# A selective-scan and mixture-of-experts kernel: scans of two segments at once, carries injected by GpSimd, and a new order of the slots

## The reference

```
u, z   = split(xn @ W_in.T)                      # 512 channels each
u_c    = silu(causal_conv4(u) + conv_b)
dt,B,C = split(u_c @ W_xp.T, [16, 32])           # 16 states
dt     = softplus(dt @ W_dt.T + b_dt);  A = -exp(A_log)
h_t    = exp(dt_t * A) * h_{t-1} + (dt_t * u_t) * B_t     # 512 channels x 16 states
y_t    = sum over states of h_t * C_t + D * u_t
out    = x + (y * silu(z)) @ W_out.T
logits = xf @ router_w + router_b; top 2; softmax of the two
expert: (silu(x We_gate) * (x We_up)) @ We_down, weighted, added to the token's row
```

## Time and profile before

| | us |
|---|---|
| median of 3 runs (2318.93 to 2322.07) | 2319.36 |
| the profiled execution's own time | 2327.84 |
| its span | 2325.9 |

### The profile page before, as it was taken

How to read it: one execution, slowest core, us unless ns; L and a number is a source line. 1 busy time by engine, 2 the same in 40 slices (tenths; PEclk the granted TensorE clock), 3 DMA queues, 4 the chain that set the end, 5 groups by cost and what they waited for, 6 DMA issues and landing times.

```text
span 2325.9 us, 32531 instructions
## 1 busy us (share of the span) xinstructions
PE 1795.3 (77%) x7694; PEld 923.0 (40%) x7694; DVE 1893.7 (81%) x2437; ACT 1806.5 (78%) x3753; POOL 1933.7 (83%) x1190
## 2 busy tenths in 40 slices
PE   5566768697878788797878788797878788666785
PEld 2112323153534344353434444353434344343542
DVE  0389988899889888899889888899889888999221
ACT  5888888888898788888998788888998787763332
POOL 1588897989999898999999898999999898987333
PEclk9888978797989898998989898997989898786998
DMA  1635454477777786677777786677777786797332
GB/s 57 145 83 141 105 141 109 125 177 184 169 178 178 169 213 160 170 183 184 174 175 180 163 218 157 171 183 180 176 179 178 160 221 147 183 259 221 70 49 34
DMA packets 217979, 369.34 MB, mean 159 GB/s; under 512 B 31040, under 2 KB 86592, under 8 KB 217664
## 3 DMA queue, kind: packets, MB, share of 16 engines
q1 hardware_dynamic: 192208, 333.56, 58.1%
q0 software_dynamic: 25584, 33.71, 7.5%
HBM read 285.05 MB, written 83.01 MB: 158 GB/s over the span
## 4 chain that ended last, share of the span: by engine, by line
issue 23%; POOL 23%; ACT 18%; PE 18%; DVE 9%; DMA 8%; POOLq 0%; ACTq 0%; DVEq 0%; SPq 0%
DMA out<-yt,xt 8%; POOL arena L1324 8%; DVE dA L1116 5%; PE ring L603 5%; ACT dA L979 4%; POOL arena L1332 4%; POOL out L1372 3%; POOL sorted_x L1362 2%; PE yps L697 2%; PE ring L611 2%; DVE arena L1116 2%; POOL arena L1347 2%; POOL arena L1342 1%; PE p_g L729 1%; PE ring L640 1%
## 5 line engine op out<-in xcount | busy, mean ns | idle before, releaser
L1324 POOL TENSOR_TENSOR arena<-arena,b_bc 128x2048 f32<-128x2048 f32 x256 | 998.4, 3900 | 88.3 <-PE yps L697 88.3
L979 ACT ACTIVATE dA<-arena,a_s 128x512 f32<-128x512 f32 x1024 | 680.5, 684 | 116.0 <-DVE arena L1125 69.9
L1116 DVE TENSOR_TENSOR_SCAN dA<-dA,arena 128x512 f32<-128x512 f32 x384 | 454.5, 1213 | 156.8 <-ACT dA L979 107.3
L1116 DVE TENSOR_TENSOR_SCAN dA<-dA,carry,arena 128x512 f32<-128x512 f32 x384 | 477.6, 1274 | 52.3 <-POOL arena L1324 36.2
L697 PE MATMUL yps<-arena,const_s 128*32 128x512 f32 x2048 | 320.4, 702 | 59.9 <-POOL arena L1332 35.9
L1332 POOL TENSOR_TENSOR arena<-arena,c_bc 128x511 f32<-128x511 f32 (+1 forms) x256 | 335.0, 1308 | 28.3 <-DVE arena L1116 26.5
L1125 DVE TENSOR_TENSOR arena<-dA,c_bc 128x1024 f32<-128x1024 f32 x256 | 313.6, 1225 | 8.8
L1372 POOL DMA_INDIRECT out<-yt,xt x135 | 215.0, 1592 | 115.7 <-ACT yt L1020 84.1
L595 PE MATMUL ring<-arena 128*128 128x512 f32 x488 | 265.4, 670 | 55.5 <-ACT arena L883 21.6
L729 PEld LDWEIGHTS p_g<-xT,w_e 128*128 128x128 f32 x1680 | 216.7, 209 | 127.5 <-issue 127.5
L603 PE MATMUL ring<-arena 128*128 128x512 f32 x480 | 236.8, 639 | 35.3 <-ACT arena L883 13.6
(11 more groups left out here) (171 smaller groups left out, 2973.5 us busy)
## 6 DMA issues: line engine op xcount, KB each, us to landing
arena<-dt_d SPq DMA_DIRECT2D x512, 256.0 KB
w_e<-in_w_moe SPq DMA_DIRECT2D x105, 512.0 KB, 4.7
dt_d<-arena SPq DMA_DIRECT2D x128, 256.0 KB, 2.4
w_e<-in_w_moe SPq DMA_DIRECT2D x105, 256.0 KB
xt<-sorted_x SPq DMA_DIRECT2D x135, 129.0 KB
b_bc<-bc_d SPq DMA_DIRECT2D x256, 64.0 KB, 2.4
c_bc<-bc_d SPq DMA_DIRECT2D x256, 64.0 KB, 5.3
xs<-in_x SPq DMA_DIRECT2D x16, 512.0 KB, 4.4
```

The lines of the kernel that those rows point to most:

```text
L979: act.activation(dA[:, j, :], rep_dt[:, c % 2, j, :], ACT.Exp, scale=a_s[:, n, j:j + 1]).then_inc(s_exp, 1)
L1116: return dve.tensor_tensor_scan(out_ap, dA[:, j, :], hs[:, u % 3, j, :], init, ALU.mult, ALU.add)
L1324: pool.tensor_tensor(hs[:, u % 3], rep_dtu[:, c % 2], b_bc[:, g, :].unsqueeze(1).to_broadcast([P, J, T]), ALU.mult).then_inc(s_dbu, 1)
```

## The change

1. **Scans.** `scan(u, j, out)` now runs over two segments in one 1024-wide instruction, start value always 0.0. For that, column 0 of `rep_dt` is set once to 1e30 and never loaded again (`load_rep` leaves it out), and the rates `a_s` are at most -1e-26, so the decay of each segment's first token is exp(-1e4) = 0 and the recurrence restarts there.
2. **Carries.** In an odd q, POOL's `add_carry` adds carry x (first token's decay) to column 0 of the four segments of hs, behind `drive` (it waits for it) and before the scans (new wait `s_inject`). The first decays are formed per chunk of four units: SP's `load_first` brings the first two dt values (`dt0`, eight bytes a row), POOL multiplies by the rates (`first_rates`), ACT takes the exponential (`first_decay`), POOL multiplies the carries (`first_carry`).
3. **Products.** Segments 2 and 3 are now one 1024-wide product. In 10 of 16 units DVE does it (from dA); in units n = 1, 4, 6, 12, 14, 15 (POOLED) the scan writes to hs and POOL does it. Segments 0 and 1 stay.
4. **Copies.** `keep2` and `keep3` with the extra column of the product become one `keep23`; `s_last` goes.
5. **Order.** Both scans of a unit stand in one row, then `activate`, then `weights` and `place`, then the second product. `route` runs at n = 5. POOL's `weigh` moves to the end of its slot. Decays are issued 1, 0, then 2, 3 late in the slot. SP's, PE's and POOL's items are reordered inside a slot, and MAKES, TAKES, `pieces` and one TILE_AT entry are set anew. MAKES0 and TAKES0 (first half) are unchanged.

```
-TILE_AT = [17, 20, 22, 24, 26, 28, 29, 31]
+TILE_AT = [17, 20, 22, 24, 26, 28, 30, 31]
+NEVER = 1.0e30
+SLOWEST = -1.0e-26
+POOLED = (1, 4, 6, 12, 14, 15)
...
-MAKES = {... (-11, 2): ["P0"], (-10, 3): ["D0"], (-9, 1): ["Z0"], (-8, 1): ["Z2"], (-8, 3): ["Z1"], (-7, 0): ["Z3"], (-6, 0): ["D1"], (-2, 0): ["D2"], (0, 4): ["D3"], ... (24, 0): ["K0"]}
+MAKES = {... (-11, 3): ["P0"], (-10, 3): ["D0"], (-10, 4): ["Z3"], (-8, 0): ["Z2"], (-8, 1): ["Z0"], (-8, 3): ["Z1"], (-6, 0): ["D1"], (-3, 2): ["D2"], (-1, 2): ["D3"], ... (23, 2): ["K0"]}
...
-TAKES = {... (-11, 1): ["W3"], (-11, 2): ["SU"], (-10, 1): ["P0"], ... (21, 3): ["R0"], (24, 0): ["K0"]}
+TAKES = {... (-11, 1): ["W3"], (-11, 4): ["SU"], (-10, 4): ["P0"], ... (21, 2): ["R0"], (24, 0): ["K0"]}
...
+                    skip = 1 if k == 0 else 0
                     for r in part:
-                        sp.dma_start(dst[32 * r:32 * r + 32, c % 2], src).then_inc(s[c % 2], 16)
+                        sp.dma_start(dst[32 * r:32 * r + 32, c % 2, :, skip:], src[:, :, skip:]).then_inc(s[c % 2], 16)
+            def load_first(q, c):
+                sp.wait_ge(s_dtw[c % 2], 32 * (2 * q + c // 2 + 1))
+                wait(sp, s_first, CC * (q // 2) + c - 1)
+                src = dt_d[q % 2, 0, c].rearrange("(j d) t -> d j t", j=J)
+                for r in range(R):
+                    sp.dma_start(dt0[32 * r:32 * r + 32, c % 2], src[:, :, 0:2]).then_inc(s_dt0[c % 2], 16)
...
             def weigh(u):                                   # PE
-                if q % 2 == 0:
-                    pe.wait_ge(s_last, UN * (q // 2) + n + 1)
...
-                pe.wait_ge(s_m2, u + 1)
-                pe.wait_ge(s_hp, u + 1)
+                pe.wait_ge(s_m01, u + 1)
+                if pooled(u):
+                    pe.wait_ge(s_hp, pooled_to(u))
+                else:
+                    pe.wait_ge(s_m23, kept_to(u))
...
+            def scan(u, j, out):
+                dve.wait_ge(s_exp, J * u + j + 2)
+                dve.wait_ge(s_dbu, u + 1)
+                if q % 2 == 1:
+                    dve.wait_ge(s_inject, UN * (q // 2) + n + 1)
+                return dve.tensor_tensor_scan(out.rearrange("p j t -> p (j t)"), dA[:, j:j + 2].rearrange("p j t -> p (j t)"),
+                                              hs[:, u % 3, j:j + 2].rearrange("p j t -> p (j t)"), 0.0, ALU.mult, ALU.add)
+            def weigh(u, j):
+                dve.wait_ge(s_c[g], 64 * (q + 1))
+                return dve.tensor_tensor(hs[:, u % 3, j:j + 2], dA[:, j:j + 2], c_bc[:, g, :].unsqueeze(1).to_broadcast([P, 2, T]), ALU.mult)
+            def unit_second(u):
+                if pooled(u):
+                    scan(u, 2, hs[:, u % 3, 2:4]).then_inc(s_h23, 1)
+                else:
+                    scan(u, 2, dA[:, 2:4]).then_inc(s_scan, 1)
...
+            def add_carry(u):                               # POOL
+                pool.wait_ge(s_dbu, u + 1)
+                pool.wait_ge(s_w0, CC * (q // 2) + n // G + 1)
+                pool.tensor_tensor(hs[:, u % 3, :, 0], hs[:, u % 3, :, 0], carry[:, n, :], ALU.add).then_inc(s_inject, 1)
+            def first_rates(q, c):
+                pool.wait_ge(s_dt0[c % 2], 64 * (2 * (q // 2) + c // 2 + 1))
...
+            def first_carry(q, c):
+                pool.wait_ge(s_e0, v + 1)
+                pool.wait_ge(s_carry01, UN * (q // 2) + G * c + G)
+                pool.wait_ge(s_carry23, UN * (q // 2) + G * c + G)
+                pool.tensor_tensor(carry[:, G * c:G * c + G, :], carry[:, G * c:G * c + G, :], e0[:], ALU.mult).then_inc(s_w0, 1)
...
                 if 0 <= s + 1 < UN * NQ:                    # POOL, the slot's order
                     drive(s + 1)
+                for p, c in firsts(s + 2):
+                    first_rates(p, c)
+                for p, c in firsts(s + 1):
+                    first_carry(p, c)
+                if 0 <= s + 1 < UN * NQ and (s + 1) // UN % 2 == 1:
+                    add_carry(s + 1)
...
-                if 0 <= s < UN * NQ:
-                    weigh(s)
...
+                if 0 <= s < UN * NQ and pooled(s):
+                    weigh(s)
```

More of the change, by code:

```diff
@@ L43, with pooled, pooled_to, kept_to @@
 LATE_FROM = UN * NQ + 1
-TILE_AT = [17, 20, 22, 24, 26, 28, 29, 31]
+TILE_AT = [17, 20, 22, 24, 26, 28, 30, 31]
 TAIL_AT = 9
+NEVER = 1.0e30
+SLOWEST = -1.0e-26
+POOLED = (1, 4, 6, 12, 14, 15)
+def pooled(u):
+    return u % UN in POOLED
+def pooled_to(u):
+    return sum(pooled(v) for v in range(u + 1))
+def kept_to(u):
+    return u + 1 - pooled_to(u)
 class Batch:
@@ L539, in _ @@
                 front = 0 <= q + 1 < NQ
-                for p, k in pieces(s, (-4, -1, 1, 6), (-10, -1, 3, 6)):
-                    store_dt(p, k)
-                if q >= 0 and front and n == 7 or s == -13:
-                    store_bc(q + 1)
-                if n == 4 and 0 <= q - 1 < NQ:
+                if n == 5 and 0 <= q - 1 < NQ:
                     store_x2(q - 1)
-                if n == 4 and 2 <= q + 2 < NQ:
+                if n == 6 and 2 <= q + 2 < NQ:
                     load_x(q + 2)
@@ L549, in _ @@
                     load_down(g, k)
-                for g, k in tiles_in(s + 1):
-                    load_tile(g, k)
+                for p, k in pieces(s, (-6, -1, 2, 6), (-10, -1, 3, 6)):
+                    store_dt(p, k)
                 if q >= 0 and front and n >= 12:
                     load_b(q + 1, n - 12)
+                if q >= 0 and front and n == 9 or s == -13:
+                    store_bc(q + 1)
+                if q == NQ - 1 and n in (4, 5, 6, 7, 9, 10, 13, 14):
+                    load_late((4, 5, 6, 7, 9, 10, 13, 14).index(n))
+                if front and n >= 13:
+                    load_c(q + 1, n - 13)
+                if 0 <= q < NQ and n in (0, 4, 8):
+                    load_rep(q, n // G + 1, (0, 1))
                 if s == -12:
@@ L576, in _ @@
                             no_tokens(e)
+                if q >= 0 and front and q % 2 == 0 and n == 12:
+                    load_first(q + 1, 0)
             sp.wait_ge(s_add, 16 * TILES)
@@ L1036, in _ @@
                 q, n = s // UN, s % UN
-                for p in ahead(s, 12, -9):
+                for p in ahead(s, 9, -19):
+                    totals(p)
+                for p in ahead(s, 11, -9):
                     norm_x(p)
@@ L1043, in _ @@
                         second_weight(p)
+                for g, k in tiles_in(s - 4, True):
+                    take_y(g, k)
                 for g, k in tiles_in(s - 3, True):
                     late_take(g, k)
-                for p in ahead(s, 9, -19):
-                    totals(p)
-                if 0 <= s < UN * NQ and q % 2 == 0:
-                    keep01(s)
-                if n == 3 and 0 <= q - 1 < NQ:
-                    squares(1, q - 1)
-                for g, k in tiles_in(s - 4, True):
-                    take_y(g, k)
-                if 0 <= s + 1 < UN * NQ:
-                    decay(s + 1, 0)
+                for p, c in firsts(s + 1):
+                    first_decay(p, c)
                 for p in ahead(s, 9, -16):
@@ L1063, in _ @@
                     take(item)
-                for p in range(NQ):
-                    if s == UN * (p + 1) + 7:
-                        gap_exp(p)
-                if 0 <= s + 1 < UN * NQ:
-                    decay(s + 1, 3)
                 for g, k in tiles_in(s - 3, False):
@@ L1080, in _ @@
                     decay(s + 1, 2)
-                if 0 <= s < UN * NQ and q % 2 == 0:
-                    keep3(s)
+                    decay(s + 1, 3)
+                for p in range(NQ):
+                    if s == UN * (p + 1) + 6:
+                        gap_exp(p)
+                if n == 3 and 0 <= q - 1 < NQ:
+                    norm_x2(q - 1)
                 for g, k in tiles_in(s - 1):
                     tanh(g, k)
-                if n == 3 and 0 <= q - 1 < NQ:
-                    norm_x2(q - 1)
+                if s == FIRST + 6:
+                    decay_rates()
                 if s in (FIRST + 3, FIRST + 4, FIRST + 5):
                     diagonals(s - FIRST - 2)
-                if s == FIRST + 6:
-                    decay_rates()
         @block.vector
@@ L1254, in _ @@
                         place(p)
-                if unit:
-                    unit_second(s)
-                for g, k in tiles_in(s - 2):
-                    activate(g, k)
-                if unit:
+                if unit and not pooled(s):
                     unit_last(s)
-                if unit and n in (4, 8, 12):
-                    gated(q, n // G - 1)
                 if tail and n == 0:
                     gated(q - 1, CC - 1)
-                if n == 6 and tail:
+                if n == 5 and tail:
                     route(q - 1)
@@ L1268, in _ @@
                     tables()
+                if s == FIRST + 7:
+                    rates()
+                if unit and n in (4, 8, 12):
```

(1 more changed line is left out.)

210 lines of the change are left out of this document (114 added, 96 removed), and 17 rows, old and new, of tables (MAKES, TAKES).

## The result

| | before | after |
|---|---|---|
| median of four runs each, us | 2320.7 (2318.9 to 2323.2) | 2356.5 (2353.4 to 2358.0) |
| profiled execution, its span, us | 2327.84, 2325.9 | 2353.42, 2351.6 |

The change makes the kernel 1.4% slower: ratio 1.0137, 95% interval 1.0115 to 1.016. That is a small loss, but the runs of the two kernels don't overlap.

The account below looks back on a forecast made before the run. POOL and DVE were taken to alternate as the bound. Even -3.3 and odd -1.0 give -4.3 us a pair, -34 over eight pairs: 2294 profiled, 2285 us forecast, own range 2255 to 2310, with rivals 2230 to 2345.

Parts of the forecast that it names:

- The 1024-wide scan: On DVE, a merged scan replacing two 512-wide ones was taken at 2.27 us, bounds 2.17 to 2.47.
- A pooled product's spacing: On POOL, a 1024-wide product was to take 1.96 us to the next start; the Trainium skill's figure was 2.2.
- The bare price of an `add_carry`: On POOL in odd sequences, each small dependent instruction was to cost 0.29 us, bounds 0.2 to 0.6; 16 make +4.6.
- The sort behind the scan: `pos` comes later in the unit and delays POOL's first scatter: +1.7 us a sequence, bounds 0 to 1.7.
- The place near n=5: Around W3's matmuls, silu and the earlier routing: taken as 0, bounds -3 to +3 us a sequence.
- The third rival: Eight-byte first-column transfers come late, `first_rates` holds every `drive`: odd halves lose 5 us each, 2325 us; chance 0.11.
- ACT's lighter load: ACT's four small copies a unit become two, -7.7 us in an even sequence; counted as nothing of its own.
- POOL in an odd half, "+1.9": POOL's load per odd sequence: product exchange -5.0, `add_carry` +4.6, `first_rates` and `first_carry` +2.3; bounds -2 to +7 us.
- Odd: DVE -5.1 where its turn is: DVE's saving per odd sequence, summed with POOL's +1.9 and the sort's +1.7 to -1.5 us, rounded to -1.0.
- Even: -3.3: Net gain per even sequence: POOL's -5.0 less 1.7 for the later sort; DVE's own -1.0 overlaps it.
- POOL's -5.0: Per sequence, 16 512-wide products leave POOL (16.8 us) and six 1024-wide ones come in (11.8 us).
- The second (2350 us): Rival: POOL becomes the bound, idling 3.7 us a sequence before pooled products; decides if POOL exceeds 122, DVE under 118; chance 0.21.

Follow-up runs that it names:

- experiment 5: Kernel after without any carries (part of the computation left out), plus one small unread POOL operation per odd unit, no wait: 2311.4 us, 0.9936 of the kernel before.
- experiment 6: Same as experiment 5, but the small POOL operation first waits for the end of `drive`: 2361.2 us, 1.016 of the kernel before.
- experiment 11: Kernel before with one added wait: in odd halves POOL waits for the end of its own `drive`; 2363.4 us, 1.0157 of the kernel before.
- experiment 2: Kernel after with `add_carry` moved behind the slot's `add_rows` and scatters: 2342.7 us, 1.0093 of the kernel before.
- experiment 9: Kernel after with column 0 formed by a small product ahead of `drive`; `add_carry` waits only for that product: 2346.3 us, 1.0078 of the kernel before.
- experiment 3: Kernel after with `route` back at n=6 and the gap's exponential at n=7: 2411.7 us, 1.0387 of the kernel before.
- experiment 4: Kernel after with the sort (`weights`, `place`) back ahead of the second scan: 2362.4 us, 1.0178 of the kernel before.
- experiment 7: Kernel after with four pooled products a half (n=1, 4, 6, 12) instead of six: 2364.2 us, 1.0172 of the kernel before.
- experiment 10: Kernel of experiment 9 with POOL's scatters moved behind the softplus pieces of their slot: 2354.2 us, 1.0117 of the kernel before.

## Why the prediction was wrong

**What held.** The 1024-wide scan takes 2.29 us (2.27 predicted), as DVE's timeline of the kernel after shows:
```profile
1183.32 1.22 DVE L1175 TENSOR_TENSOR arena<-dA,c_bc 128x1024 f32<-128x1024 f32 x1
1184.46 2.29 DVE L1168 TENSOR_TENSOR_SCAN dA<-dA,arena 128x1024 f32<-128x1024 f32 x1
```
A pooled product's spacing is 1.95 (1288.76 to 1290.71; 1.96 predicted, and 2.2 by the other figure that the prediction gave). The bare price of an `add_carry` is 3.89 - 3.77 + 0.15 = 0.27 (0.29 predicted); `first_rates` and `first_carry` take 0.18 and 0.37 to their successors (medians), 4 x 0.55 = 2.2 a half (2.3 predicted). The sort behind the scan costs POOL 1.6 us a half (1.7 predicted). The place near n=5 didn't move: n=5 and 6 together take 18.7 us in the kernel after and 18.6 (even) or 18.9 (odd) before, where the prediction had 0. The third rival is out: `first_rates` never waited for its transfers. ACT's lighter load shows in no wait: DVE waits 4.3 us for decays in the even window (4.4 before) and 5.0 in the odd one (2.6 before).

On the merged scans the Trainium skill ("VectorE: DVE Perf Modes", "Side-by-side: where the cycles go for N=2048 bf16") gives about 150 cycles of fixed cost an instruction; by the prediction's estimate from it each pair would save 0.16 us. An even pair gave 2.34 - 2.29 = 0.05, an odd one 2.47 - 2.29 = 0.18; the measurement decides.

**The step that failed: POOL in an odd half, "+1.9".** The prediction charged each `add_carry` as a small dependent instruction and asked how long it takes. It listed nothing that stands behind its wait. There stand indirect DMAs, and in the kernel before they start about 0.17 us behind `drive`'s end. With the wait ahead of them the idle time before them is 0.5 to 0.8 us and now and then 1.7. From `drive`'s start to the DMA's it is 3.89 + 0.81 = 4.70, where 3.98 was and the bare price of 0.27 would make it 4.25. That is 0.45 missing at each of the 72 slots with a DMA there, 32 us over the run (the idle time before these DMAs grew by 31.9), 4.0 an odd half. Experiments 5, 6 and 11 show the price of that wait with nothing else changed, 50 and 38 us; experiments 2 and 9 take most of the gap away and win 0.4 and 0.6% on the kernel after (10 and 14 us; for 2 the intervals overlap), while they add delays or instructions of their own. So in the complete kernel the hold accounts for 14 us of the loss as far as is shown; for the rest see below. That the wait holds up the DMA's preparation, which otherwise runs beside `drive`, is inferred from where the gap lies; the gap and its cause, the wait, are shown. POOL's odd half so had -5.0 + 4.3 + 2.2 + 4.0 = +5.5 instead of +1.9. The bounds, -2 to +7, held that; but they came from longer or shorter small instructions, so that the middle was taken where a missing term belonged. The half grew by less than this and the sort's 1.6 together, while POOL's wait for PE fell by 6.0.

**"Odd: DVE -5.1 where its turn is".** It did less: DVE's busy time in the odd window is 3.7 us down, and it idles 20.8 us instead of 13.1. DVE waited 11.3 us for POOL in that window, and what it saved itself is in its waits. In experiment 5, without the wait and the carries on POOL, the same DVE work gives 130.5. The odd half was predicted at -1.0 and came out at +3.9 (31/8).

**"Even: -3.3".** It was -1.5 (12/8). POOL's -5.0 is in its busy time. It went into waits: `pos` 0.5 to 3.0 us, a pooled product for its second scan (39.2 us in the whole run, 26.5 for the 512-wide ones before), and DVE still waits 6.6 for POOL. By slots (mean of five even halves) n=0, 2 and 15 grew by 1.1 to 1.3 each, n=1 shrank by 2.6 and n=10 to 14 by 3.0 together. Experiments 3, 4, 7 and 10 undid or moved one place of the new order each, and none won. That routing, sort and pooled products hang on one another, so that the wait turns up elsewhere, would explain it, but isn't shown.

**The rivals.** The second (2350 us) named the right engine and the right side and was 6.5 us off. Its sign came: POOL stood 2.9 and 2.2 us before a pooled product in the two windows. But its condition (POOL over 122 us in an odd half) didn't, with 119.6; it charged 3.7 us a half more to the wait for the second scan, of which at most 2.2 are there (12.7 us more than before, and 22.2 without a named releaser, over 16 halves), and it knew nothing of the held DMAs. That it was nearest is partly luck. The range was called one that takes in most of this rival, but it ended at 2345, below the rival's own 2350. The rival had 0.21 because the forecast took DVE and POOL as sharing the turns; the earlier trace rows had POOL at 120 and DVE at 119 of the odd half, and everything that was added went to POOL.

**Open.** Why the ninth's odd halves (134.8, mean of five) aren't at the 130.5 of experiment 5 isn't settled: it has 128 small products, eight instructions for the chunks a half, a wait a chunk and the real dependence of DVE on the carry. Of the 4.3 us, 3.1 lie in n=4, 5 and 13. Nor is it settled why a held DMA is 0.6 late mostly and 1.7 sometimes.

## What to carry to other kernels

Before an instruction with a wait goes into the stream of a loaded engine, list what stands behind it: its price can be what no longer starts in time behind it, and not its own length. A wait of GpSimd on its own last long instruction, ahead of an indirect DMA, cost 0.3 to 0.4 us of the kernel's time each time here, for an instruction of 0.2. Where two engines alternate as the bound, compare their load half by half after the change, and be slow to count the saving of the one that then waits for the other. Before an instruction is moved to DVE, or to another slot of it, look whether both its inputs lie in SBUF and a long GpSimd product runs beside it: the addition of four columns took up to 11.2 us so.

## What the runs showed of the hardware

Not expected: POOL's indirect DMA starts 0.16 us after the end of `drive`, but 0.78 us after it when POOL first waited for that end, and 0.59 us after the small instruction that did the waiting. 128 such waits take 38 to 50 us. The transfers of eight bytes a row, 18432 packets more, left the queue's share at 56.0%.

A 128x4 addition on DVE took 0.14 to 0.17 us beside no POOL product, 4.18 beside one of 3.83, and up to 11.2 beside four in a row, while DVE's 128x1024 products take 1.22 beside the same (1183.32, `drive` from 1180.53). The Trainium skill ("SBUF — State Buffer", "Who interferes with whom") says that a DVE instruction with two inputs in SBUF contends with a GpSimd instruction that reads SBUF, and one with at most one, outside its two-port modes, doesn't. The trace agrees: `hs` and `carry` lie in SBUF, and the products' `dA` lies in PSUM. L1214 of experiment 3, with both inputs in SBUF, shows it again (0.22 to 3.47 us).
